# Attention and top-2 experts on one core: smaller copy program in the attention, expert positions found group by group

## The reference

```python
q, k, v = (xn @ W.T + b).reshape(b, s, 16, 16)           # xn = layernorm(x)
attn_scores = einsum('bihd,bjhd->bhij', q, k) / scale
logits = li[:, :, None, :] + lj[:, None, :, :] + rel_b     # three relations for each pair i, j
bias = einsum('bijk,hk->bhij', softmax(logits, -1), logical_bias)
attn_weights = softmax(attn_scores + gate * bias, -1)
x = x + einsum('bhij,bjhd->bihd', attn_weights, v).reshape(b, s, d) @ Wo.T + bo

gate_logits = xs @ Wg                                      # xs = layernorm(x)
weights, sel = top_k(gate_logits, 2); weights = softmax(weights)
out_e = relu(xs @ W1[e] + b1[e]) @ W2[e] + b2[e]
x = x + sum over the two chosen experts of weights * out_e
```

## Time and profile before

| what | us |
|---|---|
| median of 3 runs | 5007.06 (5003.76 to 5009.56) |
| the profiled execution | 5018.32, of which the span 5016.4 |
| PE busy | 4458.2 (89%) |
| VectorE busy | 3821.7 (76%) |
| ScalarE busy | 3380.7 (67%) |
| POOL busy | 2057.0 (41%) |
| attention's results written by VectorE, first and last of 33 (the first holds nothing yet) | 366.3 and 4172.0 |
| first and last scatter begun | 4312.18 and 4393.95 |
| first product of the experts | 4403.43 |

### The profile page before, as it was taken

One profiled execution on the slowest core, in us unless ns is written; L12 is line 12 of the kernel. 1 busy time (PEld: TensorE's weight loads), 2 busy tenths in 40 slices (PEclk: granted clock), 3 DMA queues, 4 the chain that ended last, 5 costly groups with the idle time before them and its releaser, 6 DMA issues. The chain is left out here.

```text
span 5016.4 us, 183232 instructions
## 1 busy us (share of the span) xinstructions
PE 4458.2 (89%) x74128; PEld 3458.1 (69%) x74128; DVE 3821.7 (76%) x6309; ACT 3380.7 (67%) x4458; POOL 2057.0 (41%) x1809
## 2 busy tenths in 40 slices
PE   6459999999999999999999999999999996289992
PEld 3227777777777777777777777777777785267771
DVE  4388888888888888888888888888888843167773
ACT  2017887888787788877877787888888882044440
POOL 0114444444444444444444444444444442433335
PEclk9659999999999999999999999999999998589996
DMA  7514544544555445554454455454554456244434
GB/s 96 82 33 112 118 113 111 118 112 115 113 112 112 111 114 116 113 118 110 114 114 112 109 113 116 113 119 115 115 114 111 112 114 178 79 146 149 150 137 113
DMA packets 496919, 573.65 MB, mean 114 GB/s; under 512 B 136360, under 2 KB 369704, under 8 KB 492096
## 3 DMA queue, kind: packets, MB, share of 16 engines
q1 hardware_dynamic: 486880, 543.96, 46.5%
q0 software_dynamic: 6144, 16.79, 1.1%
q10 hardware_dynamic: 3040, 0.98, 0.1%
HBM read 305.10 MB, written 46.65 MB: 70 GB/s over the span
## 5 line engine op out<-in xcount | busy, mean ns | idle before, releaser
L734 DVE TENSOR_REDUCE b_mxp<-b_mx 128x1 f32<-128x512 f32 x4096 | 2635.4, 686 | 559.0 <-PE b_mx L835 508.9
L703 ACT ACTIVATE b_pr<-b_sc 128x1024 f32<-128x1024 f32 x2048 | 1986.5, 1021 | 697.0 <-PE b_sc L824 689.2
L814 PE MATMUL b_sc<-b_qm,kst 128*128 128x128 f16 x16384 | 1272.3, 220 | 54.3 <-ACT b_pr L703 42.0
L824 PE MATMUL b_sc<-b_cm,b_rst 112*128 112x128 f16 x16384 | 1264.5, 220 | 42.8 <-DMA b_rst<-b_rhi 35.5
L814 PEld LDWEIGHTS b_sc<-b_qm,kst 128*128 128x128 f16 x16384 | 971.6, 98 | 283.7 <-issue 229.5
L860 PE MATMUL b_acc<-b_pr,vp 128*32 128x128 f32 x32768 | 1124.1, 277 | 27.3 <-issue 26.9
L824 PEld LDWEIGHTS b_sc<-b_cm,b_rst 112*128 112x128 f16 x16384 | 1012.0, 98 | 49.4 <-DMA b_rst<-b_rhi 40.4
L860 PEld LDWEIGHTS b_acc<-b_pr,vp 128*32 128x32 f32 x32768 | 839.2, 110 | 265.2 <-ACT b_pr L703 190.2
L636 POOL TENSOR_TENSOR b_ex<-b_ex 128x512 f32<-128x512 f32 x512 | 654.7, 1279 | 680.8 <-ACT b_ex L682 680.8
L835 PE MATMUL b_mx<-kst,b_qx 64*128 64x512 f16 x4096 | 819.4, 397 | 92.1 <-DVE b_mxp L734 76.9
L642 POOL CAST b_rhi<-b_ex 128x512 f16<-128x512 f32 x512 | 312.8, 611 | 1293.0 <-ACT b_ex L690 1244.5
(11 more groups left out here) (144 smaller groups left out, 1726.0 us busy)
## 6 DMA issues: line engine op xcount, KB each, us to landing
b_dj<-key_logits SPq DMA_DIRECT2D x256, 768.0 KB, 7.9
b_rst<-b_rhi SPq DMA_DIRECT2D x2048, 64.0 KB, 3.2
b_rst<-b_rlo SPq DMA_DIRECT2D x1024, 64.0 KB, 3.1
c_w1r<-in_L_ffn_W_dram SPq DMA_DIRECT2D x23, 1024.0 KB, 4.9
c_w2r<-in_L_ffn_W_dram SPq DMA_DIRECT2D x23, 1024.0 KB, 4.8
expert_tokens<-c_zeros SPq DMA_DIRECT2D x23, 512.0 KB, 6.8
c_xb<-expert_tokens SPq DMA_DIRECT2D x23, 512.0 KB
expert_results<-c_y SPq DMA_DIRECT2D x23, 512.0 KB, 2.9
```

The costliest lines, as they stand in the source:

```text
L703: nc.scalar.activation(pr[:, jt % 2, half, :], sc[:, half].rearrange("p a b -> p (a b)"), ACT.Exp).then_inc(s["p_ready"], 1)
L734: nc.vector.tensor_reduce(mxp[:, head, part:part + 1], mx[:, (bank + ab) % MX_RING, :], AX.X, ALU.max).then_inc(s["mx_used"], 1)
L814: pe.matmul(sc[:, half, side, p * P:p * P + P], kst[:, pair, jt * P:jt * P + P], qm[:, par, :, pair, side * IS:side * IS + IS], start=(p = ...
L824: ins = pe.matmul(out, rst[:, u % 2, b, j0:j0 + P], cm[:, par, half, b], start=False, stop=(b % (NB // 2) == NB // 2 - 1), skip_group_chec ...
```

## The change

It has two parts. In the attention, tokens are laid on the partitions in another order (by_block), so that the rows of all eight token blocks can be copied at once: three copies of 128 KB for each half of a unit where there were six of 64 KB. SP's other copies are placed anew among the units: queries after the key logits of unit 2, queries for the bound in unit 3, the row bounds out and back after the key logits of unit 6. Every chunk also writes one part of expert_tokens with zeros, after the key logits of unit 4, since that tensor now has 79 blocks of 512 rows: eight for each expert, and what a full set of 23 blocks can reach beyond.

In the experts' stage the job list goes. Eight groups of four tiles pass through transposes, projection, statistics, normalising, gate, choice and position one step apart; a position is expert * 4096 + the number of earlier tokens of that expert, which is known group by group (seen holds the counts of the tiles before). POOL scatters a group as soon as its positions stand. After the last group, blocks() finds which rooms of expert_tokens are in use, and places_back() the packed rows for the gather; the fetch of a block reads its room from a register.

```diff
-PAD = NT // 2
+EB = S // TB
+ROOMS = E * EB + NBLK - EB
...
-    return tokens.rearrange("o (t s i b) d -> (o s) b i t d", s=2, i=BI, b=NB // 2)
+    return tokens.rearrange("o (t i b) d -> (o b) i t d", i=BI, b=NB)
...
+        zeros = sb("zeros", [ROOMS, 2 * D])
...
-            for side in range(2):
-                for part, t in enumerate((rhi, rlo, rhi)):
-                    row = 32 * part + BI * k
-                    sp.dma_start(rst[row:row + BI, u % 2, NB // 2 * side:NB // 2 * side + NB // 2, :],
-                                 t[IS * side:IS * side + IS, 2 * (u % 2) + k, :]).then_inc(s[f"r_in{u % 2}"], 16)
+            for part, t in enumerate((rhi, rlo, rhi)):
+                row = 32 * part + BI * k
+                sp.dma_start(rst[row:row + BI, u % 2], t[:, 2 * (u % 2) + k, :]).then_inc(s[f"r_in{u % 2}"], 16)
...
+        def sp_zero(sp, c):
+
+            sp.dma_start(xs_dram.rearrange("(n p t) d -> n p (t d)", n=NT, p=ROOMS)[bass.ds(c, 1)].rearrange("o p x -> (o p) x"),
+                         zeros[:, :].unsqueeze(1).broadcast_to([ROOMS, TB // NT // 2, 2 * D])).then_inc(s["zero_out"], 16)
...
-                        if u == 0 and k == 0 and not last:
-                            sp_q(sp, c + 1, 1 - par)
-                        if u == M_UNIT and not last:
-                            if k == 0:
-                                sp_m_out(sp, c + 1)
-                            else:
-                                sp_m_in(sp, c + 1, 1 - par)
                     if u + 4 < UNITS or not last:
                         sp.wait_ge(s["d_ready"], 32 * c + 4 * u + 12)
                         waited(sp)
                         sp_dj(sp, (u + 4) % UNITS)
                     if u == 1:
                         sp_att(sp, c)
-                        if more:
-                            sp.wait_ge(s["c_made"], 2 * c + 2)
-                            waited(sp)
-                            sp_qx(sp, c + 2, par)
+                    if u == 2 and not last:
+                        sp_q(sp, c + 1, 1 - par)
+                    if u == 3 and more:
+                        sp.wait_ge(s["c_made"], 2 * c + 2)
+                        waited(sp)
+                        sp_qx(sp, c + 2, par)
+                    if u == 4:
+                        sp_zero(sp, c)
+                    if u == M_UNIT and not last:
+                        sp_m_out(sp, c + 1)
+                        sp_m_in(sp, c + 1, 1 - par)
                     if u + 1 == UNITS and more:
...
-                pool.wait_ge(s[f"r_in{u % 2}"], 192 * (UNITS // 2 * x + u // 2))
+                pool.wait_ge(s[f"r_in{u % 2}"], 96 * (UNITS // 2 * x + u // 2))
...
                 sp.wait_ge(s["x_turned"], KC * (b - 1))
             sp.dma_start(xb[:, b % 2].rearrange("p t d -> p (t d)"),
-                         xs_dram[b * TB:b * TB + TB].rearrange("(p t) d -> p (t d)", t=BT)).then_inc(s[f"x_in{b % 2}"], 16)
+                         xs_dram.rearrange("(n p t) d -> n p (t d)", p=P, t=BT)[bass.ds(room(sp, b), 1)].rearrange("o p x -> (o p) x")
+                         ).then_inc(s[f"x_in{b % 2}"], 16)
...
-            sp.wait_ge(s["zeroed"], 1)
-            for b in range(NBLK):
-                sp.dma_start(xs_dram[b * TB:b * TB + TB].rearrange("(p t) d -> p t d", t=BT),
-                             zeros[:, :].unsqueeze(1).broadcast_to([P, BT, D])).then_inc(s["zero_out"], 16)
-            sp.wait_ge(s["blk_made"], 1)
+                    sp.dma_start(x1[BI * b:BI * b + BI, t, :], by_block(hidden)[b, :, t, :]).then_inc(s[f"h_in{q}"], 16)
+
+            sp.wait_ge(s["blk_made"], 2)
...
-            pool.wait_ge(s["pos_made"], 1)
-            pool.wait_ge(s["xn_done"], NT)
-            pool.wait_ge(s["zero_out"], 16 * NBLK)
             for t in range(NT):
+                if t % GT == 0:
+                    pool.wait_ge(s["xn_done"], t + GT)
+                    pool.wait_ge(s["pos_made"], t // GT + 1)
...
+            for t in range(GT * g, GT * g + GT):
+                nc.vector.tensor_tensor(seen[:, t + 1], seen[:, t], mask[:, t], ALU.add).then_inc(s["mask_made"], 1)
+                dve.wait_ge(s["mask_made"], t + 1)
...
+        def place(dve, g, links):
+
+            tiles = slice(GT * g, GT * g + GT)
+            dve.wait_ge(s["ranked"], g + 1)
+            nc.vector.tensor_tensor(slot[:, tiles, :], ps[:, 7, 0:GT * E].rearrange("p (t e) -> p t e", e=E),
+                                    base[:, :].unsqueeze(1).broadcast_to([P, GT, E]), ALU.add).then_inc(s["rank_read"], 1)
+            dve.wait_ge(s["rank_read"], g + 1)
+            for r in range(TOP):
+                links(nc.vector.tensor_tensor(slot_r[:, r, tiles], chosen[:, r, tiles], slot[:, tiles, :], ALU.mult), r == TOP - 1)
+            for r in range(TOP):
+                links(nc.vector.tensor_reduce(pos_f[:, r, tiles], slot_r[:, r, tiles], AX.X, ALU.add), r == TOP - 1)
+            nc.vector.tensor_copy(pos[:, :, tiles], pos_f[:, :, tiles]).then_inc(s["pos_made"], 1)
...
+            for step in range(GROUPS + 2):
+                if step < GROUPS:
+                    take_attention(dve, step)
+                    add_projection(dve, step)
+                    variances(dve, step, links)
+                if 1 <= step <= GROUPS:
+                    choose(dve, step - 1, links)
+                if step < GROUPS:
+                    normalise(dve, step, links)
+                if step >= 2:
+                    place(dve, step - 2, links)
+            blocks(dve, links)
+            shares(dve, links)
+            places_back(dve, links)
...
+            for step in range(GROUPS + 2):
+                if step < GROUPS:
+                    turn_attention(pe, step)
+                if 1 <= step <= GROUPS:
+                    turn_normalised(pe, step - 1)
+                if step < GROUPS:
+                    project(pe, step)
+                if 1 <= step <= GROUPS:
+                    gate(pe, step - 1)
+                if step >= 2:
+                    rank(pe, step - 2)
```

More of the change, by code:

```diff
@@ L950, in experts @@
         mask = sb("mask", [P, NT, E])
-        upto = [sb(f"upto{n}", [P, PAD + NT, E]) for n in range(2)]
+        seen = sb("seen", [P, NT + 1, E])
+        base = sb("base", [P, E])
         steps8 = sb("steps8", [P, 8])
@@ L989, in experts, with room @@
             s[f"picked_in{g}"] = sem(f"picked_in{g}")
-        kinds = ([("AT", j) for j in range(16)] + [("O", j) for j in range(16)] + [("XT", j) for j in range(16)]
-                 + [("G", 0)])
-        jobs = ["act" if k == "XT" or (k == "AT" and j % 2) else "dve" for k, j in kinds]
-        freed = {"act": s["act_job"], "dve": s["dve_job"]}
-        start = {k: next(n for n, (kk, _) in enumerate(kinds) if kk == k) for k, _ in kinds}
-        def before(eng, n):
-            return sum(1 for e in jobs[:n] if e == eng)
         N_W = 3
         block = ctx.enter_context(nc.Block())
+        def room(sp, b):
+            return sp.value_load(blk_r[0:1, b:b + 1], min_val=0, max_val=ROOMS - 1)
         def fetch_x(sp, b):
@@ L1190, in split_x @@
+            for r in range(TOP):
+                links(nc.vector.tensor_tensor(pos_f[:, r], pos_f[:, r], diff[:, :] if r else e_diff[:, :], ALU.add), r == TOP - 1)
+            nc.vector.tensor_copy(back[:, :, :], pos_f[:, :, :]).then_inc(s["back_made"], 1)
         def split_x(dve, b):
@@ new lines, in turn_normalised, with gate @@
+        def turn_normalised(pe, g):
+            pe.wait_ge(s["xn_done"], GT * g + GT)
+            if g:
+                pe.wait_ge(s["xnT_done"], KC * g)
+            for c in range(KC):
+                for t in range(GT):
+                    ins = pe.transpose(ps[:, 4 + c, t * P:t * P + P], a[:, GT * g + t, c * P:c * P + P], ident[:, :])
+                ins.then_inc(s["xn_turned"], 1)
+        def gate(pe, g):
+            pe.wait_ge(s["xnT_done"], KC * g + KC)
+            if g:
+                pe.wait_ge(s["lg_read"], g)
+            for t in range(GT):
+                tile = GT * g + t
+                for c in range(KC):
+                    ins = pe.matmul(ps[:, 6, t * E:t * E + E], aT[:, c, tile * P:tile * P + P], wgs[:, c, :],
+                                    start=(c == 0), stop=(c == KC - 1))
+            ins.then_inc(s["gated"], 1)
@@ new lines, in rank @@
+        def rank(pe, g):
+            pe.wait_ge(s["mask_made"], GT * g + GT)
+            if g:
+                pe.wait_ge(s["rank_read"], g)
+            tiles = slice(GT * g, GT * g + GT)
+            pe.matmul(ps[:, 7, 0:GT * E], earlier[:, :], mask[:, tiles, :].rearrange("p t e -> p (t e)"), start=True, stop=False)
+            pe.matmul(ps[:, 7, 0:GT * E], ones[:, :], seen[:, tiles, :].rearrange("p t e -> p (t e)"), start=False,
+                      stop=True).then_inc(s["ranked"], 1)
```

299 lines of the change are left out of this document (150 added, 149 removed).

## The result

The changed kernel takes 6477.93 us (median of 4 runs, 6457.07 to 6485.01) against 5005.41 of the kernel before on the same chip: 1.2935 times as long, 95% interval 1.2903 to 1.2968. The profiled execution took 6485.01 us, 1466.7 more than the profiled one before. The time is inside the range of the prediction and 3 us from its forecast of 6475.

What follows compares the result with a forecast made beforehand. PE, busy 89% of the span, was taken as the bound, so its stalls add to the total. 5018.3 + 173 + 1360 - 64 = 6487, against the median 6476, said as 6475; range 5080 to 6740.

Steps and rivals of the forecast that it cites:

- queries out of unit 0: Attention: query copies no longer split the b_rst copies; PE's 34.8 us wait and about 4 clock drops go, -43 us.
- row bounds late, with the clock: Attention, unit 6: bounds queued behind key logits delay PE 5.2 us in 31 chunks, +161 us; slow clock after stalls, +55.
- zeros on one engine: Attention: each chunk's zeros take 50 us on one DMA engine, b_rst waits behind; 32 x 42.5 = +1360 us; chance 0.78.
- front: Start of the expert stage: eight group steps of 13.9 us, last scatter ends near 4329 instead of 4395; -64 us.
- divisor rule: DMA copies: engine count is the common divisor up to 16 of both sides' outer counts; 632 and 79 give one.
- "interleaved" rival: Attention zeros: one engine, but packets interleaved with b_rst's, so PE stands only a few microseconds; about 5200 to 5500; chance 0.04.
- Zeros on sixteen engines: 5116: Attention rival: zeros spread over sixteen engines and hidden, row bounds still late; 5116 us (5050 to 5175); chance 0.12.

## Why the prediction was right

Forecast 6475, measured 6478. By its own steps, in us, "a chunk" for the difference of the profiles times 32, "median" for that of the medians:

| step | predicted | measured | from |
|---|---|---|---|
| queries out of unit 0 | -43 | -69 (a chunk), -46 (median) | queries moved alone |
| row bounds late, with the clock | +216 | +186 (a chunk), +198 (median) | row bounds late alone |
| zeros on one engine | +1360 | +1395 (profiles), +1367 (medians) | rest: 1511.7 + 69 - 186, or 1472.5 + 46 - 198 + 46 |
| front | -64 | -46 | the two profiles |
| sum | +1469 | +1466 | |

The measured sum agrees with the total by construction, since the zeros' term is what the others leave. It also holds what the three b_rst copies in place of six are worth, which the prediction put at 0 and no run shows alone. The direct check of it is the wait: 39.2 us a chunk where 40 were forecast.

- **Zeros.** Mechanism and size hold: one engine, 26 GB/s, 50 us, a stall of up to 40.4 where 40 was forecast, the half clock for some 6 us behind it (1152.85 to 1159.21) and so some 3 us lost where 2.5 were forecast, b_rst on PE at 1152.85, 71 us after the unit's start near 1082 where 69 was. The divisor rule, then read from two copies, held for 79, 74 and 16. That b_rst lies behind the zeros on their engine holds only within one queue: from ScalarE's queue the same zeros let b_rst pass. The "interleaved" rival was false for SyncE's one queue and true for two.
- **Row bounds.** Landing 6.8 (7.1 forecast) and 1.6 (2.4), POOL's wait 8.6 in the mean, PE's stall 5.8: as forecast. Of the +186 of the run with the row bounds late alone, 141 are longer waits of PE (182.8 - 42.0) and 45 the rest, the clock among it; 161 and 55 were forecast.
- **Queries.** The wait went and did not come again. The sign and the cause hold; -69 to -46 against -43. The profile of the kernel before was 11 us over its median, so -46 is the better figure.
- **Front.** Mis-sized by 18 us. The first scatters of the first six groups are 14.7, 17.4, 17.5, 17.5 and 16.1 us apart and not 13.9 each, 14 us more in all; the rest is a start 3 us later and slightly longer scatters. The sum of a step's parts was right (13.7 with no scatter running); what it left out is a hole of 2.1 to 3.3 us at each of four groups of scatters.
- **The rival that would have been wrong.** "Zeros on sixteen engines: 5116" has the right cause and probably the wrong price. With the zeros on sixteen engines the kernel takes 5379, 263 us more: I had called 3.5 us of copies hidden because b_rst had room, and had not asked who else needs the DMA engines. That run has packets of 1 KB, and its zeros landed after 17.6 us once the row bounds were early; packets of 2 KB on sixteen engines were not run, so how far 5116 would have been off is open.

The errors of the terms partly cancel: -26, -30, +35 and +18 by the profiles, -3, -18, +7 and +18 by the medians. Either way the 3 us between forecast and result are luck; by the medians the terms are good to some 20 us each. The range of 5080 to 6740 is wide, and a result inside it says little by itself; the stall seen in the trace says more.

## What to carry to other kernels

Read the outer counts of both sides of each new copy. By the rule that 79, 74 and 16 bear out, with a prime over 16 in one of them it runs on one engine and holds everything behind it on its queue, so cut it into rows of sixteen. A large background copy belongs in small pieces between the others even when it is spread, since the engines' waits for "issue" grow behind a burst. A change with several parts is worth splitting: here moving the queries alone gives 0.9%, and the whole with zeros in eight spread copies of long rows, early row bounds and spread queries 1.5%, where all together in their first form cost 29%.

## What the runs showed of the hardware that was not expected

- A copy behind a one-engine copy of 632 packets keeps the issuing engine itself for 45.81 us (43.1 to 46.3 in the first eight chunks read); with two engines the second of the zeros' copies kept it 21.26 us. From ScalarE's queue the one copy a chunk took 0.71 us to issue.
- PE stopped up to 9.8 us for "issue" in the run with zeros of 16 rows, and between equal products with no semaphore, while a burst of copies ran; in the kernel before the longest such wait is 2.7 us.
- Narrow copies of two queues (zeros on one engine, queries on two) cost more than a narrow and a wide one: 338 us of PE's waits for b_rst against 2.1.
- Around the end of a group of eight indirect scatters there are 2.1 to 3.4 us in which VectorE and ScalarE get no start; with the scatters held back there are none. Why is open.
